# Graph network on one core: more prefilled fetch buffers, a new order of full and fetched tiles, and the W2 split moved out of the edge stages

## The reference

```python
def _gine_layer(x, src, dst, edge_attr, eps, We, be, W1, b1, gamma, beta, W2, b2):
    e = edge_attr @ We + be
    m = jax.nn.relu(x[src] + e)
    agg = jax.ops.segment_sum(m, dst, num_segments=x.shape[0])
    h = ((1.0 + eps) * x + agg) @ W1 + b1
    mu = jnp.mean(h, axis=0)
    var = jnp.mean(jnp.square(h - mu), axis=0)
    h = (h - mu) * jax.lax.rsqrt(var + BN_EPS) * gamma + beta
    h = jax.nn.relu(h)
    return jax.nn.relu(h @ W2 + b2)
```

## Time and profile before

| | |
|---|---|
| median of three runs | 971.86 us |
| the profiled execution: its own time | 970.5 us |
| its span | 968.6 us |
| mean granted TensorE clock | 0.921 |
| PE busy | 841.4 us, 87% |
| DVE busy | 712.1 us, 74% |
| ACT busy | 516.6 us, 53% |
| POOL busy | 281.5 us, 29% |

### The profile page before, as it was taken

How to read it: one execution, slowest core, us unless ns; L and a number is a source line. 1 busy time by engine, 2 the same in 40 slices (tenths; PEclk the granted TensorE clock), 3 DMA queues, 4 the chain that set the end, 5 groups by cost and what they waited for, 6 DMA issues and landing times.

```text
span 968.6 us, 13328 instructions
## 1 busy us (share of the span) xinstructions
PE 841.4 (87%) x3561; PEld 603.7 (62%) x3561; DVE 712.1 (74%) x1275; ACT 516.6 (53%) x986; POOL 281.5 (29%) x245
## 2 busy tenths in 40 slices
PE   2989779887869789995999989999999999999796
PEld 2667345655647567773665865667656766658664
DVE  8997825765876677786888668976799758986535
ACT  2376103544646241514786567755677557764445
POOL 3000653865200000015352075502654045520000
PEclk9989657989969799997999999999999999999898
DMA  5412454676433312208676077841978138860101
GB/s 113 142 38 87 115 161 154 178 225 193 151 99 157 129 45 64 84 26 217 148 187 180 3 202 179 200 119 33 240 177 217 37 108 197 178 165 1 43 1 53
DMA packets 59286, 122.20 MB, mean 126 GB/s; under 512 B 9096, under 2 KB 22698, under 8 KB 59221
## 3 DMA queue, kind: packets, MB, share of 16 engines
q0 software_dynamic: 20048, 52.18, 22.6%
q1 hardware_dynamic: 36581, 64.56, 22.6%
q10 hardware_dynamic: 2592, 4.61, 1.3%
HBM read 105.60 MB, written 15.73 MB: 125 GB/s over the span
## 4 chain that ended last, share of the span: by engine, by line
PE 67%; DVE 17%; ACT 8%; issue 5%; another core or an unknown queue 2%; DMA 1%; SPq 0%; ACTq 0%; DVEq 0%
PE ps L996 15%; PE ps L973 10%; PE ps L671 9%; PE ps L1012 6%; PE ps L1028 6%; PE ps L797 4%; PE ps L862 3%; PE ps L919 3%; PE ps L776 2%; PE ps L663 2%; ACT slot_recs L1090 2%; PE ps L765 2%; DVE z_parts L1864 1%; DVE w L1391 1%
## 5 line engine op out<-in xcount | busy, mean ns | idle before, releaser
L996 PE MATMUL ps<-z_parts,onehot_dst 128*125 128x512 f32 x664 | 205.2, 414 | 5.6 <-DVE z_parts L1864 2.9
L1864 DVE SCALAR_TENSOR_TENSOR z_parts<-ps,z_parts 128x512 fp32r<-128x512 f32 x216 | 147.9, 688 | 43.4 <-ACT z_parts L1296 31.0
L671 PE MATMUL ps<-w,xT 128*125 128x512 f32 x660 | 174.7, 419 | 5.1 <-DVE w L1391 5.1
L1296 ACT ACTIVATE z_parts<-ps 128x512 fp32r<-128x512 f32 x216 | 128.7, 597 | 80.9 <-PE ps L973 66.9
L973 PE MATMUL ps<-x_parts,gather_lhs 128*128 x432 | 142.4, 415 | 22.5 <-DVE x_parts L1831 12.1
L996 PEld LDWEIGHTS ps<-z_parts,onehot_dst 128*125 128x125 f32 x664 | 110.0, 186 | 72.8 <-issue 55.0
L671 PEld LDWEIGHTS ps<-w,xT 128*125 128x125 f32 x660 | 129.8, 200 | 37.7 <-issue 6.8
L639 POOL DMA_INDIRECT queued<-node_rows,srci x60 | 96.0, 1600 | 93.7 <-ACT queued L1245 76.8
L653 POOL TENSOR_TENSOR work<-x_cur,be_rows 125x512 f32<-125x512 f32 x20 | 25.5, 1282 | 317.7 <-ACT x_cur L1059 188.9
L973 PEld LDWEIGHTS ps<-x_parts,gather_lhs 128*128 128x128 f32 x432 | 80.3, 193 | 56.5 <-issue 40.2
L633 POOL DMA_INDIRECT gathered<-rel_rows,rowi x79 | 85.7, 1084 | 51.4 <-DVE gathered_parts L1623 22.0
(11 more groups left out here) (275 smaller groups left out, 1154.7 us busy)
## 6 DMA issues: line engine op xcount, KB each, us to landing
w_stage<-in_weights SPq DMA_DIRECT2D x88, 256.0 KB
onehot_dst<-onehot_rows SPq DMA_DIRECT2D x80, 250.0 KB
onehot_rows<-onehot_dst ACTq DMA_DIRECT2D x18, 250.0 KB
gather_lhs<-edge_src_rows SPq DMA_DIRECT2D x8, 432.0 KB, 7.4
node_rows<-work SPq DMA_DIRECT2D x20, 160.0 KB, 2.0
queued<-node_rows,srci POOLq DMA_INDIRECT x116
node_rows<-work SPq DMA_DIRECT2D x20, 90.0 KB, 2.0
rel_rows<-rel_rows_out SPq DMA_DIRECT2D x10, 160.0 KB, 1.9
```

What stands on the lines that cost most here:

```text
L671: mm = pe.matmul(ps[0:R, bank, :], lt[:, a, k, n * R:(n + 1) * R], w[:, b, k, :], start=first and k == 0 and (a, b) == THREE[0], stop=last ...
L996: mm = pe.matmul(ps[0:R, d, :], S[:, j // SK % SR, j % SK, :], Z[:, g % ZR, a, :], start=False, stop=False, skip_group_check=True)
L1296: nc.scalar.activation(Z[:, g % ZR, HI, :], of, ACT.Relu).then_inc(z_hi, 1)
L1864: v.scalar_tensor_tensor(out=Z[:, g % ZR, LO, :], in0=of, scalar=0.0, in1=Z[:, g % ZR, HI, :].bitcast(F32), op0=ALU.max, op1=ALU.subtract) ...
```

## The change

1. QR goes from 10 to 16. Ten buffers stay where they were, and six lie in the region of the edge counts, which is free by then. Their semaphores are those of the R-GCN stage's fetches.
2. The first sixteen fetched tiles of a layer are all prefilled by ACT and fetched with an accumulating DMA; from the seventeenth on they alternate as before. A layer has 23 sets and 6 adds, before 15 and 14.
3. A mixed group has the order full, full, fetched, fetched, full.
4. The sets have new places. Two stand between the W1 jobs of the layer before, nine after the split of the next W1, five at steps 2 to 10 of the edge stage. For the first layer five stand after the last L1 weights and six among the last L1 rows.
5. W2 is split in the node stage: ACT after three transposed tiles, DVE between its node tiles.
6. In the node stage PE transposes three tiles, runs the first W1 job, transposes the other two and goes on.
7. x + be of the layers after the first is made by DVE from ps, right after the low part, and no longer by POOL from X. ACT's plain rows wait for it.
8. SP loads the row We ahead of w_load(14 + 2l).

```diff
--- before.py
+++ after.py
@@ -41,7 +41,8 @@
 MR = 4
-QR = 10
+QR = 16
+QL = 10
 NREC = 4
@@ -53,7 +54,8 @@
 LAG = 3
-EARLY = 10
+SET_W1, SET_W2 = 2, 11
+SET_AT = (2, 4, 6, 8, 10)
 HI, LO = 0, 1
@@ -72,17 +74,17 @@
 ROWS = ((0, 80), (80, R))
-W2_HIGH, W2_LOW = (24, 26, 28, 30), (28, 31, 34, 37)
...
     a, b = LEAD + 3 * q, TF + 2 * q
-    ORDER += [a, b, a + 1, b + 1, a + 2]
+    ORDER += [a, a + 1, b, b + 1, a + 2]
 ORDER += range(TF + TL // 2 * 2, TE)
 STEP = {t: i for i, t in enumerate(ORDER)}
-SETS = (TL + 1) // 2
-ADDS = TL // 2
+MIXED = TL // 2
+SETS = QR + (TL - QR + 1) // 2
+ADDS = TL - SETS
 NG = -(-TE // SK)
@@ -216,9 +218,10 @@
         L0 = L1.bitcast(F32)
-        Q = [at(l_at, TF * P * 4 + 2048 * i, f"queued{i}", [P, D]) for i in range(QR)]
-        BEB = at(l_at, TF * P * 4 + 2048 * QR, "be_rows", [P, D])
-        WEB = at(l_at, TF * P * 4 + 2048 * (QR + 1), "we_rows", [P, D])
+        Q = [at(l_at, TF * P * 4 + 2048 * i, f"queued{i}", [P, D]) for i in range(QL)]
+        Q += [at(a_at, APAD * 4 + 2048 * i, f"queued{QL + i}", [P, D]) for i in range(QR - QL)]
+        BEB = at(l_at, TF * P * 4 + 2048 * QL, "be_rows", [P, D])
+        WEB = at(l_at, TF * P * 4 + 2048 * (QL + 1), "we_rows", [P, D])
         SS = at(l_at, 0, "onehot_src_b", [P, 2, CG, P], BF16)
...
@@ -387,7 +391,7 @@
         q_set = sem("queue_rows_set")
-        q_in = [sem(f"queue{i}_in") for i in range(QR)]
+        q_in = gath[GA:GA + QR]
         x_kept = sem("x_kept")
@@ -438,6 +442,19 @@
             return 16 if i < GA else 16 * ((i - GA) // GR + 1)
+
+        def prefilled(k):
+            return k < QR or (k - QR) % 2 == 0
+
+        def sets(k):
+            return sum(prefilled(j) for j in range(k + 1))
+
+        def adds(k):
+            return k + 1 - sets(k)
+
+        def queue_landed(l, k):
+            before = (TE - GA - 1 - k % QR) // GR + 1
+            return 16 * (before + l * ((TL - 1 - k % QR) // QR + 1) + k // QR + 1)
@@ -568,13 +585,14 @@
                     s_load(l, g)
+                if l < NL2 - 1:
+                    sp.wait_ge(q_set, SETS * (l + 1))
+                    sp.wait_ge(q_add, ADDS * (l + 1))
+                    web_load(l + 1)
                 w_load(14 + 2 * l)
...
                         s_load(l + 1, g)
-                    sp.wait_ge(q_set, SETS * (l + 1))
-                    sp.wait_ge(q_add, ADDS * (l + 1))
-                    web_load(l + 1)
                     sp.wait_ge(ht_done, 8 * (l + 1))
@@ -634,23 +652,19 @@
                 row = bass.IndirectOffsetOnAxis(ap=srci[:, k:k + 1], axis=0)
-                if k % 2 == 0:
-                    gp.wait_ge(q_set, SETS * l + k // 2 + 1)
+                if prefilled(k):
+                    gp.wait_ge(q_set, SETS * l + sets(k))
                     gp.indirect_dma_start(Q[k % QR][:, :], None, xb_d, row, compute_op=ALU.add)\
...
                 else:
-                    if k >= QR:
-                        gp.wait_ge(z_made, l * TE + STEP[TF + k - QR] + 1)
+                    gp.wait_ge(z_made, l * TE + STEP[TF + k - QR] + 1)
                     gp.indirect_dma_start(Q[k % QR][:, :], None, xb_d, row).then_inc(q_in[k % QR], 16)
+            gp.wait_ge(beb_in, 16)
+            for n in range(NT):
+                gp.wait_ge(x_made, XM_L3 - NT + n + 1)
+                gp.tensor_tensor(H[0:R, n, :], X[0:R, n, :], BEB[0:R, :], ALU.add).then_inc(xb_made, 1)
             for l in range(NL2):
-                gp.wait_ge(beb_in, 16 * (l + 1))
-                for n in range(NT):
-                    if l:
-                        gp.wait_ge(x_kept, NT * (l - 1) + n + 1)
-                    else:
-                        gp.wait_ge(x_made, XM_L3 - NT + n + 1)
-                    gp.tensor_tensor(H[0:R, n, :], X[0:R, n, :], BEB[0:R, :], ALU.add).then_inc(xb_made, 1)
                 gp.wait_ge(xb_out, 32 * NT * (l + 1))
@@ -998,11 +1012,18 @@
                     close(b).then_inc(acc_done, 1)
-                for n in range(NT):
+
+                def g_transposes(n):
                     pe.wait_ge(g_made, l * NT + n + 1)
                     transposes(n, H[0:R, n, :])
+
+                for n in range(3):
+                    g_transposes(n)
                 pe.wait_ge(w_split, wpieces(WJ_L2[l]))
                 for i, (o, h) in enumerate(HJOBS):
+                    if i == 1:
+                        g_transposes(3)
+                        g_transposes(4)
                     if i == 0:
@@ -1257,7 +1278,7 @@
                 if l == NL1 - 1:
-                    for k in range(0, EARLY, 2):
+                    for k in range(5):
                         queue_set(0, k)
@@ -1272,38 +1293,40 @@
                 normal(X[0:R, n, :], H[0:R, n, :], NT + n, NT + n + 1, x_made)
+                for k in range(5 + n + n // 2, 6 + n + (n + 1) // 2 if n < NT - 1 else 0):
+                    queue_set(0, k)
             act.wait_ge(o_done, NT * NL1)
...
             for l in range(NL2):
-                k = EARLY
+                k = QR
                 for i, t in enumerate(ORDER):
...
                     else:
-                        c = l * ((TL - 1 - (t - TF) % QR) // QR + 1) + (t - TF) // QR + 1
-                        if (t - TF) % 2 == 0:
-                            act.wait_ge(q_in[(t - TF) % QR], 16 * c)
+                        if prefilled(t - TF):
+                            act.wait_ge(q_in[(t - TF) % QR], queue_landed(l, t - TF))
                         else:
-                            act.wait_ge(q_add, ADDS * l + (t - TF) // 2 + 1)
+                            act.wait_ge(q_add, ADDS * l + adds(t - TF))
                         of = Q[(t - TF) % QR][:, :]
...
                     nc.scalar.activation(Z[:, g % ZR, HI, :], of, ACT.Relu).then_inc(z_hi, 1)
+                    if i in SET_AT:
+                        queue_set(l, SET_W2 + SET_AT.index(i))
                     while k < TL and STEP[TF + k] - 14 <= i:
...
                         nc.scalar.copy(B[0:R, n, :], X[0:R, n, :]).then_inc(b_made, 1)
-                    if i in W2_HIGH:
-                        w_high(13 + 2 * l, W2_HIGH.index(i))
-                for n in range(NT):
+                for n in range(3):
                     tr_high(n, GT, n, TR_L2[l] + n + 1)
+                w_highs(13 + 2 * l)
@@ -1318,20 +1341,25 @@
                                          ACT.Identity, bias=colt[:, 0, l, o:o + 1]).then_inc(ht_raw, 1)
+                    if i == 0:
+                        for n in range(3, NT):
+                            tr_high(n, GT, n, TR_L2[l] + n + 1)
                     if i >= 2:
                         (h_high if i % 2 else root_h)((i - 2) // 2)
-                    if l < NL2 - 1 and 2 * i < EARLY:
-                        queue_set(l + 1, 2 * i)
+                    if l < NL2 - 1 and i < SET_W1:
+                        queue_set(l + 1, i)
                 root_h(KT - 1)
...
                 if l < NL2 - 1:
+                    for k in range(SET_W1, SET_W2):
+                        queue_set(l + 1, k)
                     for n in range(NT + 1):
...
                         if n:
-                            act.wait_ge(xs_made, NT * (l + 1) + n)
+                            act.wait_ge(xb_made, NT * (l + 1) + n)
                             nc.scalar.activation(X[0:R, n - 1, :], ps[0:R, n - 1, :], ACT.Relu).then_inc(x_kept, 1)
@@ -1576,11 +1604,13 @@
             w_lows(3)
-            mixed = dlo[:, LEAD:LEAD + 5 * ADDS].rearrange("p (q m) -> p q m", m=5)
+            mixed = dlo[:, LEAD:LEAD + 5 * MIXED].rearrange("p (q m) -> p q m", m=5)
             v.tensor_copy(dlo[:, 0:LEAD], dlf[:, 0:LEAD])
-            v.tensor_copy(mixed[:, :, 0:5:2], dlf[:, LEAD:TF].rearrange("p (q m) -> p q m", m=3))
-            v.tensor_copy(mixed[:, :, 1:5:2], dlf[:, TF:TF + 2 * ADDS].rearrange("p (q m) -> p q m", m=2))
-            link(v.tensor_copy(dlo[:, LEAD + 5 * ADDS:TE], dlf[:, TF + 2 * ADDS:TE]))
+            full = dlf[:, LEAD:TF].rearrange("p (q m) -> p q m", m=3)
+            v.tensor_copy(mixed[:, :, 0:2], full[:, :, 0:2])
+            v.tensor_copy(mixed[:, :, 4:5], full[:, :, 2:3])
+            v.tensor_copy(mixed[:, :, 2:4], dlf[:, TF:TF + 2 * MIXED].rearrange("p (q m) -> p q m", m=2))
+            link(v.tensor_copy(dlo[:, LEAD + 5 * MIXED:TE], dlf[:, TF + 2 * MIXED:TE]))
@@ -1844,21 +1874,18 @@
             def queue_add(l, k):
-                if k == 1:
-                    v.wait_ge(web_in, 16 * (l + 1))
-                v.wait_ge(q_in[k % QR], 16 * (l * ((TL - 1 - k % QR) // QR + 1) + k // QR + 1))
+                v.wait_ge(web_in, 16 * (l + 1))
+                v.wait_ge(q_in[k % QR], queue_landed(l, k))
                 v.scalar_tensor_tensor(out=Q[k % QR][:, :], in0=WEB[:, :], scalar=wt[:, TF + k:TF + k + 1],
...
             for l in range(NL2):
-                k = 1
+                k = QR + 1
                 for i, t in enumerate(ORDER):
...
                         k += 2
-                    if i in W2_LOW:
```

(20 more changed lines are left out.)

3 lines of the change are left out of this document (2 added, 1 removed).

## The result

The changed kernel takes 976.9 us in the median against 971.7 for the kernel before, both on the same chips: a ratio of 1.008, with an interval from 1.006 to 1.010. Ratios and intervals in this text are formed from the fast runs alone and can differ a little from the quotient of two medians, here 1.005. The changed kernel is slower by 0.8% by this ratio, where a median of 958.5 was forecast, with a range from 948 to 975. The profiled execution spans 972.2 us against 968.6.

What follows compares the result with a forecast made beforehand. PE bounds the edge stages, with stalls behind z_parts from DVE's adds in a tight loop. Edge stages -22.0, boundaries +6.5 and L1 rows +2.2 give -13.3 from 970.5, so 957.2; median 958.5, range 948 to 975.

Steps and rivals of the forecast that it cites:

- part 1: Edge stages: fewer adds and a new tile order put eight groups at 3.80 us, five at 4.15; 6.2 less a layer.
- Part 2: W2 split moved from edge to node stage: no edge-stage term of its own, 0 in the node stage.
- part 5: Edge-stage DMA: eight fetches a layer become accumulating, 1.55 us of all engines each; late arrivals cost 0.7 us a layer.
- four rivals: Other outcomes: slack too tight 20%, DVE's work returning whole 8%, dearer fetches 10%, sets and W2 split reaching further 10%.
- latency rival: Edge stages: 0.16 us of slack doesn't hold, the first eight groups stay at 4.15; 966.7 us, chance 20%.
- the slack of 0.16: Mixed group without an add: PE reaches the first full tile's scatter at 2.33 us, and it is ready at 2.17.
- DVE's occupancy: Edge stages: the work taken off DVE, 8.0 us, comes back whole; 948.6 us, chance 8%.
- Part 3: Layer end: nine sets ahead of the x_parts high parts start PE 2.15 us later at three boundaries, +6.5.
- Part 4: Last L1 rows: six sets between rows, one costing 0.25 us and two 0.87; 2.2 us, once.
- DMA rival: Edge stages: accumulating fetches dearer than 1.55 us when packed densely; at 2.1 they end 6.6 late, 982 us; chance 10%.

Runs made afterwards that it cites:

- with registers: 17 tile words loaded into PE registers once instead of in each edge stage: changed kernel ratio 0.989, same edit in the kernel before 0.988.
- both mendings: Changed kernel with tile words held in registers and seven sets instead of two between the W1 jobs: 927.5 us, ratio 0.980 to the kernel before.

## Why the prediction was wrong

**Step that failed: part 1, the eight groups at 3.80.** The step before it, that 4.42 less 3.72 is a loop of gather, ACT, DVE and scatter that misses its slack by DVE's add, was read from one place in the timeline (two groups at 610 to 616) and taken for all thirteen. It is true of that place: without loads the kernel before has 4.14 in most groups, the changed kernel 3.8 without an add and 4.14 with one, and without adds these too go to 3.8. But in the trace as it was, seventeen register loads a stage were a second cause, of which the prediction has no word: the term put them at nothing without a reason. The thirteen pitches of the four stages were forecast at 204.8 us and took 226.9. Of the 22.1 too many the loads are 17.1; the other 5.0 are left with registers (209.8). The gain was forecast as 24.8; measured are 3.6 with the loads and 15.1 without.

The loads also cost the kernel before 5.6 us, which the step booked on the adds. And its 4.42 is a mean over unlike groups: the three with the W2 split take 5.0, 4.3 to 4.4 and 5.1 to 5.2, the others 4.0 to 4.9. Part 2 said that the split was in the 4.42, and so it was.

Of the 5.0 us left with registers, 2.05 are late one-hot rows (see part 5), and some 0.5 falls together with ACT's copies in group eight of the first layer (4.31). The rest is not explained.

None of the four rivals had the loads. The latency rival had 4.15 for the early groups; they took 4.43, and not by its mechanism: the slack of 0.16 does hold in most of them once the loads are gone. Nor was DVE's occupancy the measure: 6.3 busy us less in the stage gave 1.6. The Trainium skill (Perfetto Trace Analysis, Identifying the Most-Contended Engine) has the engine of highest occupancy optimised first, which pointed to DVE; in the changed kernel the adds' removal moved no time, and in the mended one it took 4.6 us off the edge stages.

**Part 3, the boundary: right, and short by the clock.** Forecast 2.15 at each of three, 6.5; from the last W2 matmul to the first gather it is 4.67 instead of 2.48, 2.19 at each, 6.6. The node stages lost 7.3: 2.0, 3.3 and 2.0. With seven sets between the jobs it is gone. What the step left out is that PE then runs its first matmuls, or those from the fourth on, at 1.2 GHz. In the measured difference this is small, since the kernel before also did so in two of these three leads (12.8, 11.0 and 13.1, against 12.7, 12.6 and 13.0 after). Only the experiments show what it costs.

**Part 2, the split of W2 in the node stage: right.** Forecast 0. The first and third node stages are 2.0 longer, of which the boundary is 2.19, so the split gave back 0.2. The second stage has 1.3 more, and it is the one in which the granted clock is below 1.00 (windows view of the second and third node stage, the clock third from the end):

```profile
638.03:678.51 40.48, 33.91 (x181) 29.24 (x182) 29.80 (x64) 26.53 (x50) 0.00 (x0) 0.96 0.24 72
755.47:794.60 39.13, 32.53 (x181) 27.87 (x182) 29.81 (x64) 26.56 (x50) 0.00 (x0) 1.00 0.25 74
```

**Part 4, the L1 rows: right in kind, too dear.** Forecast 2.2. From normal to normal the row behind one set takes 5.39 as before (418.31 to 423.70), that behind two 5.80 against 5.32 (423.70 to 429.50), and the four rows 22.15 against 21.16: 1.0 in all. One set costs nothing instead of 0.25, since ACT's next wait for DVE's statistics shrinks (3.38 to 2.90), and two cost 0.48 instead of 0.87 (that wait goes from 3.31 to 2.69).

```profile
423.70 0.81 ACT L1080 ACTIVATE x_cur<-work,nmr,rstd 125x512 f32<-125x512 f32 x1 [0.59 <-DVE nmr L1714]
424.42 1.32 ACT L1266 ACTIVATE queued<-we_rows,wt 128x512 f32<-128x512 f32 x2
425.65 0.28 ACT L1074 ACTIVATE sd<-mv,eps_deg 125x1 f32<-125x1 f32 x1
428.62 0.29 ACT L1074 ACTIVATE sd<-mv,epst 125x1 f32<-125x1 f32 x1 [2.69 <-DVE mv L1698]
```

**Part 5, DMA: the price was right, and so was the size of the cost, by late one-hot rows.** The queue rows of 574 to 590 (packets, MB, share of 16 engines):

```profile
q0 software_dynamic: 1212, 2.21, 81.9%
q1 hardware_dynamic: 621, 1.10, 21.6%
```

2.21 MB are 8.4 fetches, and 0.819 x 16 = 13.1 us: 1.55 each, as computed. The engines are full there, and yet neither ACT nor PE ever waits for a fetched tile. PE does wait for one-hot rows, though. One of the two longest pitches of the changed kernel, 5.47 in layer 3, has this stall (timeline of PE, then the source view of PE's wait for the rows, 705 to 707):

```profile
706.60 0.72 PE L1010 MATMUL ps<-z_parts,onehot_dst 128*125 128x512 f32 x2 [1.41 <-DVE z_parts L1891]
...
L1008 PEldq EVENT_SEMAPHORE  x1: 51/51/51, 706.2 to 706.2; - x1
```

The row names DVE, but the z of that tile had been ready since 703.95. The group of one-hot rows landed at 706.17 (by the trace's semaphore events), PE's wait for it (L1008) ended at 706.2, and three register operations and the scatter followed. Counted so, from the later of z and the instruction before the wait to the landing, late rows cost the four stages nothing in the kernel before (0.7 with registers), 1.5 us in the changed kernel, 2.05 with registers and 2.75 with both mendings, where two of them (0.88 and 1.04) make the pitches of 4.83 and 5.10. With plain fetches there are none. The forecast had 2.8.

Crowding may also lengthen the loads of words: the four loads of this stage that took 0.54 to 0.93 us lie between 579 and 594, where the DMA share is 1.01 to 1.07, and from 595 on none is over 0.40; and with plain fetches the sum over all stages fell by 5.6 us. But the longest load of the changed kernel, 0.98 at 492.8, falls where the share is 0.72 (492 to 494.5), there are loads of 0.30 in the crowded stretch, and the plain fetches changed much else. So the cause of the long ones is not shown. The rule that queues of all engines interleave on the same DMA engines (the Trainium skill, DMA: Bandwidth & Descriptors, Issuing engines are not separate DMA queues) agrees with the shares of q0 and q1, which sum to 1.04, and its consequence, late one-hot rows, did come, though at a tenth or so of the lateness that the DMA rival reckoned with (4 x 6.6 us at 2.1 a fetch).

## What to carry to other kernels

Before a stall is put down to the engine that is named last, look at what the stalled engine's own sequencer does in the gap: rows of register loads, moves and address operations appear in no busy share, and here PE, only some 0.5 us behind its sequencer, felt them. Look also at the engine's other waits there: a late DMA hid behind a row that named DVE. Values that steer a loop and don't change belong in registers loaded once, in a stretch where the engine waits anyway; that alone was worth 1.2% in the one kernel and 1.9% in the other. And when a bound engine gets relief, list what else lies under its stalls, since that comes to the surface and takes the gain.
